# The output projection and the first FFN product in fp32r pieces, in a new order of the pipeline, with the next layer's weights prepared partly on GpSimd

## The reference, cut to what matters

```
x_before = x;  x = layernorm(x)
DEPTH, HEADS, DIM_HEAD, WINDOW = 6, 16, 64, 32
INNER, DIM_INNER = 1024, 341
for i in range(DEPTH):
    # attention
    q, k, v = split(shift_tokens(x) @ Wqkv[i])               # 128 -> 3 x 1024
    q = rotary(l2norm(q) * q_scale[i]);  k = rotary(l2norm(k) * k_scale[i])
    out = softmax(8 * q @ k.T + mask) @ v                    # windows of 32 tokens, each looks at 64
    x = out @ Wo[i] + x                                      # output projection, 1024 -> 128
    # FFN
    xn = layernorm(shift_tokens(x)) * ln_g[i] + ln_b[i]
    a, gate = split(xn @ W1[i] + b1[i])                      # first FFN product, 128 -> 2 x 341
    x = (a * gelu(gate)) @ W2[i] + b2[i] + x                 # second FFN product
x = x_before + x
```

## Time and profile before

| | us |
|---|---|
| median of 3 runs | 3593.33 |
| lowest and highest | 3586.91, 3593.59 |
| the profiled execution, its own time | 3582.8 |
| its span | 3579.8 |
| PE busy in the span | 3386.0 (95%) |
| DVE, ACT, POOL busy | 3116.5, 2507.2, 1846.9 |

### The profile page before, as it was taken

One profiled execution on the slowest core, in us unless ns is written; L12 is line 12 of the kernel. 1 busy time (PEld: TensorE's weight loads), 2 busy tenths in 40 slices (PEclk: granted clock), 3 DMA queues, 4 the chain that ended last, 5 costly groups with the idle time before them and its releaser, 6 DMA issues.

```text
span 3579.8 us, 150019 instructions
## 1 busy us (share of the span) xinstructions
PE 3386.0 (95%) x63524; PEld 2724.3 (76%) x63524; DVE 3116.5 (87%) x6016; ACT 2507.2 (70%) x4543; POOL 1846.9 (52%) x1604
## 2 busy tenths in 40 slices
PE   5767999999999999999999999999999999999997
PEld 2325888877888887788887888887788887888885
DVE  8987888888888888888888888888888889888884
ACT  2015777777777777777777777777777777777774
POOL 1434555655555555456555455555565564555561
PEclk9988999999999999999999999999999999999999
DMA  2002433333333333433232433332432332333333
GB/s 85 12 27 53 95 76 83 73 66 78 91 83 79 69 75 74 95 83 75 65 83 59 110 79 71 73 81 58 113 76 63 83 79 61 81 72 70 83 78 82
DMA packets 186825, 267.79 MB, mean 75 GB/s; under 512 B 31670, under 2 KB 89908, under 8 KB 185396
## 3 DMA queue, kind: packets, MB, share of 16 engines
q1 hardware_dynamic: 186164, 258.24, 32.0%
HBM read 22.30 MB, written 4.19 MB: 7 GB/s over the span
## 4 chain that ended last, share of the span: by engine, by line
PE 86%; issue 7%; DVE 4%; ACT 1%; POOL 1%; SPq 1%; DMA 0%; DVEq 0%; POOLq 0%; ACTq 0%
PE bank L668 10%; PE bank L655 10%; PE bank L720 9%; PE obank L702 8%; PE bank L753 7%; PE bank L631 7%; PE bank L633 5%; PE bank L632 5%; PE bank L678 5%; PE bank L712 4%; PE bank L646 3%; PE bank L760 3%; PE bank L648 2%; PE bank L647 2%; PE bank L740 2%
## 5 line engine op out<-in xcount | busy, mean ns | idle before, releaser
L978 POOL TENSOR_TENSOR qn<-qn,rinv 128x512 f32<-128x512 f32 x768 | 796.5, 1053 | 1310.0 <-DVE rinv L1225 1310.0
L972 POOL TENSOR_TENSOR qn<-ropec,ropes 128x512 f32<-128x512 f32 x768 | 990.5, 1304 | 203.4 <-DVE ropes L1177 156.2
L853 ACT ACTIVATE sq<-bank 128x512 f32<-128x512 f32 x768 | 456.2, 599 | 151.8 <-PE bank L633 107.9
L1176 DVE TENSOR_TENSOR ropec<-bank,rots 128x512 f32<-128x512 f32 x768 | 523.7, 682 | 17.2 <-ACT sq L853 10.3
L1185 DVE TENSOR_REDUCE ss<-sq 128x8 f32<-128x512 f32 x768 | 496.8, 676 | 41.8 <-ACT sq L853 41.8
L1177 DVE TENSOR_TENSOR ropes<-bank,rots 128x512 f32<-128x512 f32 x768 | 521.8, 679 | 0.0
L655 PE MATMUL bank<-ident,qn 128*128 128x128 f32 x3072 | 469.7, 276 | 19.2 <-ACT qT L871 11.8
L668 PE MATMUL bank<-kT,qT 64*32 64x64 f32 x24576 | 430.9, 217 | 18.4 <-issue 13.5
L668 PEld LDWEIGHTS bank<-kT,qT 64*32 64x32 f32 x24576 | 368.1, 107 | 102.0 <-issue 80.2
L655 PEld LDWEIGHTS bank<-ident,qn 128*128 128x128 f32 x3072 | 368.1, 141 | 87.9 <-POOL qn L978 27.8
L631 PE MATMUL bank<-wqkv_hi,xs_hi 128*128 128x512 f32 x768 | 363.5, 473 | 27.3 <-issue 18.6
(11 more groups left out here) (138 smaller groups left out, 6275.6 us busy)
## 6 DMA issues: line engine op xcount, KB each, us to landing
V<-Vt SPq DMA_DIRECT2D x576, 260.0 KB, 4.5
V<-Vt SPq DMA_DIRECT2D x192, 130.0 KB, 4.6
V<-Vt SPq DMA_DIRECT2D x192, 65.0 KB, 4.1
xres<-X SPq DMA_DIRECT2D x96, 128.0 KB, 2.1
X<-x SPq DMA_DIRECT2D x96, 128.0 KB, 2.1
wqkv_raw<-L_ffn_Wqkv SPq DMA_DIRECT2D x6, 1536.0 KB
xraw<-X SPq DMA_DIRECT2D x97, 64.0 KB
xraw<-X SPq DMA_DIRECT2D x97, 63.8 KB
```

The costliest lines, as they stand in the source:

```text
L972: pool.tensor_tensor(qn[:, c, :], ropec[:, c % ROPE_RING, :], ropes[:, c % ROPE_RING, :], ALU.add).then_inc(rope_sum.sem, 1)
L978: pool.tensor_tensor(heads8(qn[:, c, :]), heads8(qn[:, c, :]), rinv[:, 8 * c:8 * c + 8].unsqueeze(2).broadcast_to([P, 8, DH]), ALU.mult).t ...
L1176: dve.tensor_tensor(halves(ropec[:, c % ROPE_RING, :]), raw, table(t, 2 * kind), ALU.mult)
```

## The change

Four things change. `wo` and `w1` become three fp32r products for each fp32 one. Their operands get a high part (ACT copy: `oh` of the attention output, a second copy after `xn`, and the weights' copies write the high part) and a low part on POOL (`ol`, `xl`, and `wd` for the weights). The conversion for the next layer moves: the thirds of Wqkv are converted at fixed places of the last round of the old layer (after `proj.7` and `v.1` on ACT, after `add.6` and `norm.5` on POOL) and of the first round of the new one (after `proj.1` and `add.2`), each once the projections that read that third are done, with the low parts and the rotary tables on POOL instead of DVE; only the first layer's are still made by DVE ahead of the pipeline. And the four word lists are new. Some buffers of the first stage move (`OTf` to `Vt`, `pick` to `OT`), and the fill of `Vt` moves behind that stage.

```diff
 ORDER = {
     "pe": """
-        proj.0 proj.1 tr.2' pt.3'' w1.1''' tr.3' ot.1'' pv.3'' ...
+        w1.0''' tr.1' pv.2'' proj.0 proj.1 tr.2' w1.1''' pt.3'' ...
...
+        EDGE = {"act": {"last": {("proj", 7): 0, ("v", 1): 1}, "first": {("proj", 1): 2}},
+                "pool": {"last": {("add", 6): 0, ("norm", 5): 1}, "first": {("add", 2): 2}}}
...
 def c_wo(c, _, layer):                                   # PE
+    pe.wait_ge(w_clo, 2 * layer + 1)
+    pe.wait_ge(ot_lo_done.sem, ot_lo_done.at(c, 4))
     for i in range(8):
-        mm = pe.matmul(b_c[:, 0:T], wo[:, i, :], OT[:, i, :], start=i == 0, stop=i == 7)
+        pe.matmul(b_c[:, 0:T], wo_hi[:, i, :], OT_hi[:, i, :], start=i == 0, stop=False)
+        pe.matmul(b_c[:, 0:T], wo_lo[:, i, :], OT_hi[:, i, :], start=False, stop=False)
+        mm = pe.matmul(b_c[:, 0:T], wo_hi[:, i, :], OT_lo[:, i, :], start=False, stop=i == 7)
...
 def c_w1(c, j, layer):                                   # PE
-        mm = pe.matmul(b_c[0:n, part * T:(part + 1) * T], w1[:, cols], xn[:], start=True, stop=True)
+        pe.matmul(o, w1_hi[:, cols], xn_hi[:], start=True, stop=False)
+        pe.matmul(o, w1_lo[:, cols], xn_hi[:], start=False, stop=False)
+        mm = pe.matmul(o, w1_hi[:, cols], xn_lo[:], start=False, stop=True)
...
 def b_ot(b, u):                                          # ACT
+    act.wait_ge(ot_lo_done.sem, ot_lo_done.at(b, u - 1) if u >= 2 else ot_lo_done.at(b - 1, u + 3))
+    act.activation(OT[:, u % 2], b_trB[:].rearrange("p (j q) -> p j q", j=4),
+                   ACT.Copy).then_inc(ot_copied.sem, 1)
+def b_oh(b, u):
+    act.wait_ge(ot_copied.sem, ot_copied.at(b, u + 1))
+    act.activation(OT_hi[unit], OT[:, u % 2], ACT.Copy).then_inc(ot_hi_done.sem, 1)
...
 def c_ln_(c, n, layer):                                  # ACT
+    act.wait_ge(c_xn.sem, c_xn.at(c, 1))
+    act.activation(xn_hi[:], xn[:], ACT.Copy).then_inc(xn_hi_done.sem, 1)
...
+def b_ol(b, u):                                          # POOL
+    pool.wait_ge(ot_hi_done.sem, ot_hi_done.at(b, u + 1))
+    pool.tensor_tensor(OT_lo[unit], OT[:, u % 2], OT_hi[unit].bitcast(F32), ALU.subtract).then_inc(ot_lo_done.sem, 1)
+def c_xl(c, _):
+    pool.wait_ge(xn_hi_done.sem, xn_hi_done.at(c, 1))
+    pool.tensor_tensor(xn_lo[:], xn[:], xn_hi[:].bitcast(F32), ALU.subtract).then_inc(xn_lo_done.sem, 1)
+def w_low(c, layer, k):
+    if k == 0:
+        pool.wait_ge(w_c, 4 * layer + 1)
+        pool.tensor_tensor(wo_lo[:], wo_raw[:], wo_hi[:].bitcast(F32), ALU.subtract).then_inc(w_clo, 1)
+    else:
+        pool.wait_ge(w_c, 4 * layer + 3)
+        pool.tensor_tensor(w1_lo[:], w1_raw[:], w1_hi[:].bitcast(F32), ALU.subtract).then_inc(w_clo, 1)
+def w_a(layer, k):
+    if k == 0:
+        pool.wait_ge(roped.sem, roped.at(layer * NB, 8))
+        rotary_scaled(pool).then_inc(rots_done, 1)
+    cols = slice(k * W_THIRD, (k + 1) * W_THIRD)
+    pool.wait_ge(w_hi, 3 * layer + k + 1)
+    pool.tensor_tensor(wqkv_lo[:, cols], wqkv_raw[:, cols], wqkv_hi[:, cols].bitcast(F32), ALU.subtract).then_inc(w_lo, 1)
...
-            pipeline(dve, lambda *z, **k: run_slots(steps, "dve", *z, **k), conv_a)
+            pipeline(dve, lambda *z, **k: run_slots(steps, "dve", *z, **k))
```

More of the change, by code:

```diff
@@ L293, in la_pipeline, with pipeline @@
             channels(LA_STEPS, 0, [], True)
-        def pipeline(eng, body, conv_a=None, loads=None):
+        def pipeline(eng, body, loads=None):
             body(1, 0, (0,), 0, None)
@@ L306, in pipeline @@
                 for g in range(3, NB):
-                    body(l * NB + g + 1, g, (0, 1, 2, 3), None, {2: l, 3: l})
-                conv_a and conv_a(l + 1)
-                body(l * NB + NB + 1, 0, (0, 1, 2, 3), l + 1, {2: l, 3: l})
+                    body(l * NB + g + 1, g, (0, 1, 2, 3), None, {2: l, 3: l},
+                         edge=("last", l + 1) if g == NB - 1 else None)
+                body(l * NB + NB + 1, 0, (0, 1, 2, 3), l + 1, {2: l, 3: l}, edge=("first", l + 1))
                 body(l * NB + NB + 2, 1, (0, 1, 2, 3), None, {2: l, 3: l}, (2, l + 1))
@@ L331, in run_slots @@
                     continue
-                if kind == "wa":
-                    if layer is not None and not is_first(layer):
-                        step(layer, i)
-                    continue
-                if kind == "wc":
+                if kind in ("wc", "wd"):
                     if conv_c is not None and conv_c[0] == lag:
@@ L354, in run_slots @@
                         step(n - lag, i)
+                if edge is not None and lag == 0 and engine in EDGE:
+                    third = EDGE[engine][edge[0]].get((kind, i))
+                    if third is not None:
+                        steps["third"](edge[1], third)
                 if end == 2 and lag in (0, 2) and engine in FIN_AFTER:
@@ L395, in build @@
         W_THIRD = INNER
+        THIRD_READ = [1 + max(PROJ_ORDER.index(("proj", c)) for c in range(8) if chunk(c)[0] == kind) for kind in range(2)] + [12]
         @block.sync
@@ L478, in place_v, with body @@
                     move(half, 0, 0, P - WIN, slice(1, 2), WIN)
-            def body(n, g, lags, layer, c_layers, conv_c=None, end=0):
+            def body(n, g, lags, layer, c_layers, conv_c=None, end=0, edge=None):
                 has_a, has_b, has_c, has_d = (lag in lags for lag in (0, 1, 2, 3))
@@ L519, in loads @@
                 hold(sp, sp_held, w_c, 4 * layer)
+                hold(sp, sp_held, w_clo, 2 * layer)
                 load_weights(layer)
@@ L746, in c_w1 @@
                 if j == 0:
-                    pe.wait_ge(w_c, 4 * layer + 3)
-                    pe.wait_ge(c_xn.sem, c_xn.at(c, 1))
+                    pe.wait_ge(w_clo, 2 * layer + 2)
+                    pe.wait_ge(xn_lo_done.sem, xn_lo_done.at(c, 1))
                 else:
@@ L803, in row_norm @@
                 if not first:
-                    conv_a(0)
-                    w_a(0, 1)
-                    w_a(0, 2)
+                    for k in range(3):
+                        w_a(0, k)
                 for k in range(8):
@@ L950, in _ @@
                 w_cs(0, 0, k)
-            steps.update({"wa": w_a, "wc": w_cs})
-            pipeline(act, lambda *z, **k: run_slots(steps, "act", *z, **k), conv_a)
+            steps.update({"third": w_a, "wc": w_cs})
+            pipeline(act, lambda *z, **k: run_slots(steps, "act", *z, **k))
         @block.gpsimd
@@ L1170, in a_proj @@
                 n = PROJ_ORDER.index(("proj", c))
+                if c == 0 and layer is not None and not is_first(layer):
+                    dve.wait_ge(rots_done, layer)
                 dve.wait_ge(squared.sem, squared.at(a, c + 1))
```

97 lines of the change are left out of this document (55 added, 42 removed).

## The result

The changed kernel takes 3528.02 us (median of 4 runs, 3523.87 to 3532.33) against 3590.12 (4 runs, 3583.43 to 3593.59): a ratio of 0.9828, interval 0.9812 to 0.9844. It is faster, by 62 us where 135 were forecast.

The account below looks back on a forecast made before the run. PE was taken to bound the kernel, busy throughout plain rounds. From the profiled 3582.8 us, -128 (plain rounds), -12 (edges) and +4 (ends) gave 3446.8; with 10.5 for the median 3457, rounded 3458; range 3415 to 3545.

Parts of the forecast that it names:

- Output projection: On PE, 24 fp32r products at a pitch of 0.118 us replace the fp32 block, saving 0.62 us a round.
- Rival A: Slower: halving the columns doesn't halve the product; pitch from 0.150 us on decides for it, 3884 us; chance 0.04.
- First FFN product: On PE, three w1 blocks of 4 instructions become three of 6 at 0.118: 2.59 to 2.12, saving 0.47 us.
- Order: New PE order: two pairs of row-tiled blocks adjoin in a round instead of one, saving 0.33 us.
- Who must keep up: Plain round: PE work 31.53 us, other engines close behind; 0.07 added for 31.6, saving 128 us over 95 rounds.
- My walk over the queues: Following the new order's queues once round: DVE comes round in about 31.5 us, POOL has 1.2 us of slack.
- Rival B: Faster but less: DVE or POOL comes late in the plain round; round 32.5 us, time 3542; chance 0.15.
- Layer edge: Conversions moved from DVE, largely to POOL: an edge costs 8.9 instead of 11.3 us, 12 saved over five.
- the 4 us of the forecast: PE wait at the layer edge: POOL's second and third thirds take 5.0 us against 1.2 of slack.
- Ends: Draining rounds +3.5 us for new hops nothing hides, start 0 to 4 for POOL's first low parts; +4 in all.

Follow-up runs that it names:

- experiment 6: The kernel before with only the change's four word lists; its own fp32 products and its conversions on DVE stay: 3548.93 us, ratio 0.9895.
- run 8: The changed kernel with only the high x high products of wo and w1, those with low parts left out: 3508.41 us.
- Experiment 1: The changed kernel with one word of POOL's list moved: wd.1, the low part of w1, made behind add.6: 3489.77 us, ratio 0.9732.
- experiments 4 to 6: 4: change with conversions in POOL's gap, loads spread over ten rounds, 3444.89 us; 5: kernel before, loads spread, 3578.89; 6: kernel before, new order, 3548.93.

## Why the prediction was right in direction and wrong in size

The change is faster by 62 us where 135 were forecast. The plain rounds got shorter by the mechanism that was forecast; what failed is the step on the layer edge. By its steps:

1. **Output projection: right.** Pitch 0.116 for 0.118; like for like, in the new order, the block is 0.64 us shorter for 0.62. Rival A (a pitch of 0.150 or more) is out. The Trainium skill's rule (TensorE: Matmul & The Clock Gate, The mechanism), that a weight load overlaps a running product only when the row group differs, is not borne out: 24 products of full height with a load each take 2.90 us. The same section also lets a load run ahead when it goes to the background weight buffer, which these numbers would fit.
2. **First FFN product: mis-sized.** 0.29 for 0.47 like for like (2.60 to 2.31); where such a block follows an fp32 transpose its first product takes 0.20, not 0.12.
3. **Order: nearly.** 0.27 for 0.33, by experiment 6. Part of it shows at the start of the `wo` and `w1` blocks.
4. **Who must keep up: mis-sized.** The plain round was to be 31.6 and is 31.87. PE's own work is 31.65, not 31.53; and the small waits are 0.2, not 0.07. 95 times the difference is 26 us. My walk over the queues gave DVE a round of 31.5, and run 8 puts the loop of the others at about 31.6 when PE is relieved, so the walk was good; wrong was to add two terms this close almost as if the larger alone decided. POOL did take 24.0 us. DVE is busy for 28.44 us, 89% of the round, where I had 29.38 unchanged and 94 to 95% (29.38 of 31.5 is 93%); why it got less isn't known. Rival B, a round of 32.5, did not come: the changed plain round has no recorded wait of PE.
5. **Layer edge: failed, and this is the main error.** Forecast -12 us, measured +48. I counted POOL's busy time ("The two following rounds have 2.5 and 1.7 us more on POOL: 1.5 and 0.7 us of wait") and put the wait at the excess over its slack. For the third and fourth intervals that made 11 us over the five edges; they have 57.8, where the kernel before had 7.6. The step asked how much more POOL does, not by when PE needs it: `wd.1` ends POOL's round, `w1.0` begins PE's next, and 6.79 us of idle PE plus 2.1 of slow clock follow. Experiment 1 gave 34 to 38 us back by that word alone. The other miss is that I left the 20 loads at nothing, as in the kernel before they nearly are (5.7 us over five intervals): in the new order the same burst costs 19.7 plus 7.6 in the first layer (experiments 4 to 6). Where I did count a deadline, the second and third thirds of Wqkv against the output projection, the first interval came out at 27.7 for a forecast of 33.5. The idle time in it, 3.9 us, is the 4 us of the forecast, but only 1.87 of it is recorded as a wait for POOL's low part of a third, at the projection; the rest is mainly 1.0 for the mask copy and 0.9 in front of `wo`.
6. **Ends: small.** +4 forecast, -1.7 measured.

The measured time does lie in the stated range of 3415 to 3545, but that is luck: the upper part of the range was there for rival B, and what brought the time up to it is the edge.

The miss of 84 us between the profiled executions is then 60 at the edges, 26 in plain rounds and 6 in the first layer, less 7 elsewhere. With the two causes of step 5 taken out and the conversions in POOL's gap, the kernel runs at 3444.89 us, near my 3458. That is no confirmation: its edges are better (23 us for 44.5) and its plain rounds worse than my sum had them.

## What to carry to other kernels

When work moves to another engine, compare for each moved piece the moment it is reached with the moment its first reader wants it, in the new order of both; busy time and slack over a round say nothing of that, and work that is done once a layer shows in no plain round. A piece with a deadline belongs into the engine's wait, not behind its last word. When the bounding engine gets shorter, look again at everything that cost nothing before, bursts of loads too; and once the other engines' loop is nearly as long as the bounding engine's work (31.63 and 31.65 us here), relief of one alone gives little.
